# A two-layer image kernel on one core: the reciprocal root from bits and Newton steps, matrix halves made on GpSimd, and the small chains laid out over other half slots

## What is computed

```python
def _gn(v, G=32, eps=1e-5):                     # groups of 4 channels
    g = v.reshape(B_, G, C_ // G, H_, W_)
    m = jnp.mean(g, axis=(2, 3, 4), keepdims=True)
    s = jnp.var(g, axis=(2, 3, 4), keepdims=True)
    return ((g - m) / jnp.sqrt(s + eps)).reshape(v.shape)

# layer 0, of _gn(x)
xh = _conv1x1(x, w_in, b_in)                    # 128 -> 256 channels
pooled = jnp.mean(xh, axis=(2, 3))
hcx = jax.nn.relu(pooled @ kg_w1.T + kg_b1)
kernels = (hcx @ kg_w2.T + kg_b2).reshape(b, c, K, K)
y = conv_general_dilated(x_r, k_r, ...)         # 3x3, each channel its own kernel
y = y * jnp.tanh(jax.nn.softplus(y))            # Mish
return _conv1x1(y, w_out, b_out)                # 256 -> 128 channels

# layer 1, of _gn(x), for each pixel: real FFT over channels, mask, two
# 128 x 128 products, inverse FFT, real part, relu
x = x + layer0(_gn(x))
x = x + layer1(_gn(x))
```

## Time and profile before

| | |
|---|---|
| time, three runs | 3999.41, 4001.52, 4002.96 us (median 4001.52) |
| the profiled execution | 4002.64 us, of which the span of its instructions 4000.8 us |
| busy: PE | 3806.2 us (95%) |
| busy: ACT | 3597.6 us (90%) |
| busy: DVE | 3518.9 us (88%) |
| busy: POOL | 2549.2 us (64%) |
| DMA queues | 30.5% of 16 engines' span |
| chain that ended last | PE 69%, ACT 14%, DVE 8%, issue 5%, POOL 2%, DMA 1% |

### The profile page before, as it was taken

One profiled execution on the slowest core, in us unless ns is written; L12 is line 12 of the kernel. 1 busy time (PEld: TensorE's weight loads), 2 busy tenths in 40 slices (PEclk: granted clock), 3 DMA queues, 4 the chain that ended last, 5 costly groups with the idle time before them and its releaser, 6 DMA issues.

```text
span 4000.8 us, 65640 instructions
## 1 busy us (share of the span) xinstructions
PE 3806.2 (95%) x22348; PEld 2274.3 (57%) x22348; DVE 3518.9 (88%) x4714; ACT 3597.6 (90%) x5827; POOL 2549.2 (64%) x1812
## 2 busy tenths in 40 slices
PE   4899999999999999999999999999999999999998
PEld 2555555555565555655556555555655555555554
DVE  5899989899898988989889898998989889898996
ACT  4889999899998999999999998999989999998885
POOL 2456666666666666666666666666666666666763
PEclk8999999999999999999999999999999999999999
DMA  3212333333333333333333232333323333332222
GB/s 134 59 48 79 111 96 111 100 106 111 96 111 101 106 106 101 111 101 106 101 106 111 96 111 96 111 106 101 111 96 107 104 103 114 97 109 76 74 75 121
DMA packets 111291, 401.85 MB, mean 100 GB/s; under 512 B 13232, under 2 KB 14320, under 8 KB 110704
## 3 DMA queue, kind: packets, MB, share of 16 engines
q1 hardware_dynamic: 110960, 397.66, 30.5%
HBM read 263.39 MB, written 134.22 MB: 99 GB/s over the span
## 4 chain that ended last, share of the span: by engine, by line
PE 69%; ACT 14%; DVE 8%; issue 5%; POOL 2%; DMA 1%; SPq 0%; ACTq 0%; POOLq 0%; DVEq 0%
PE psA L686 31%; PE psBO L732 17%; PE psL L741 9%; ACT tprod L425 4%; DVE accB L929 4%; DVE accS L941 3%; PE psBO L710 2%; PE psBO L712 2%; PE psBO L711 2%; ACT xh L398 2%; ACT tprod L474 2%; PE psBO L721 1%; ACT XS L462 1%; PE psBO L722 1%; PE psBO L723 1%
## 5 line engine op out<-in xcount | busy, mean ns | idle before, releaser
L686 PE MATMUL psA<-hi,wa 128*128 128x288 f16 (+4 forms) x9792 | 1951.5, 282 | 0.8 <-DVE wtmp L911 0.8
L929 DVE SCALAR_TENSOR_TENSOR accB<-xh,vectors,accB 128x1024 f32<-128x1024 f32 x1280 | 1643.6, 1284 | 0.0
L1102 POOL TENSOR_TENSOR tsum<-tsum,tprod 128x1024 f32<-128x1024 f32 x512 | 1209.8, 2363 | 393.8 <-ACT tprod L425 393.5
L941 DVE SCALAR_TENSOR_TENSOR accS<-side,vectors,accS 128x448 f32<-128x448 f32 x2048 | 1403.8, 685 | 22.4 <-ACT accS L434 13.2
L686 PE MATMUL psA<-lo,wa 128*128 128x288 f16 (+5 forms) x4896 | 1330.6, 281 | 0.0
L686 PEld LDWEIGHTS psA<-hi,wa 128*128 128x128 f16 x9792 | 931.4, 98 | 340.3 <-issue 68.9
L732 PE MATMUL psBO<-wm,woutt 128*128 128x512 f32 x2048 | 963.5, 593 | 2.9 <-DVE X L951 2.1
L1106 POOL TENSOR_TENSOR X<-X,zt 128x512 f32<-128x512 f32 x480 | 610.8, 1273 | 485.8 <-DVE accB L929 408.7
L1094 POOL TENSOR_TENSOR lo<-X,hi 128x1024 f16<-128x1024 f32 x256 | 546.8, 2136 | 405.0 <-ACT hi L383 403.6
L732 PEld LDWEIGHTS psBO<-wm,woutt 128*128 128x128 f32 x2048 | 386.5, 190 | 483.0 <-issue 481.9
L425 ACT ACTIVATE tprod<-xh,vectors 128x1024 f32<-128x1024 f32 x512 | 584.0, 1141 | 21.0 <-POOL tsum L1102 18.3
(11 more groups left out here) (166 smaller groups left out, 3582.7 us busy)
## 6 DMA issues: line engine op xcount, KB each, us to landing
X<-in_x_dram SPq DMA_DIRECT2D x256, 512.0 KB, 3.5
out_dram<-X SPq DMA_DIRECT2D x256, 512.0 KB, 2.6
XS<-in_x_dram SPq DMA_DIRECT2D x240, 512.0 KB, 3.5
X<-in_w_t_dram SPq DMA_DIRECT2D x2, 1152.0 KB, 17.7
w1t<-in_w_t_dram SPq DMA_DIRECT2D x1, 256.0 KB, 2.7
wint<-in_w_in_t_dram SPq DMA_DIRECT2D x1, 128.0 KB, 2.3
woutt<-in_w_out_t_dram SPq DMA_DIRECT2D x1, 128.0 KB, 2.6
wm<-in_cos_m_dram SPq DMA_DIRECT2D x1, 64.0 KB, 4.3
```

The lines of the kernel that those rows point to most:

```text
L686: last = mm(o[:, r:r + q, 0:cols], w, src[:, at:at + q, SIDE + dx - 1:SIDE + dx - 1 + cols], start=(tap == ORDER[0] and w is wh and src is ...
L929: V.scalar_tensor_tensor(out=rows_of(accB[:]), in0=xh[:, 8 * j + dy:8 * j + dy + 8, dx:dx + W], scalar=kk[i % 2][:, TAPS + k:TAPS + k + 1] ...
L941: V.scalar_tensor_tensor(out=side_out(), in0=side[:, 8 * j + dy:8 * j + dy + 8, dx:dx + SIDE], scalar=kk[i % 2][:, k:k + 1], in1=side_out( ...
L1102: P.tensor_tensor(tsum[:], tsum[:], tprod[:], ALU.add).then_inc(s_ta, 1)
```

## The change

It has four parts, in words, and then the diff cut to its core.

1. **The reciprocal root.** `stats_rstd` (ACT: Ln, Exp with scale -0.5) is gone. DVE makes a first guess from the bits of the variance (`root_bits`: shift right by one; `root_first`: a constant minus that), and `rstd` on POOL makes three Newton steps in place of one, 15 instructions in place of 7. ACT uses no function outside Mish's table any more.
2. **Halves on POOL.** `weights_high` and `taps_high` (ACT) are gone; POOL copies and subtracts (`weights_halves`, `taps_halves`).
3. **Chains sooner and spread.** The chain of x begins in slot 10. `rstd` and `fold` run at the end of POOL's slot 11; `pooled_products` moves to `small_0` of slot 12 and `hidden` to `small_1` of slot 12; `kernels` to `small_0` and `bias_rows` to `small_1` of slot 13; the three `spread`s to `small_0` and `small_1` of slot 14 and `small_0` of slot 15. For layer 1, `rstd` and `fold_1` move to the end of POOL's slot 2 and `layer1_mean` to `small_0` of slot 3. On POOL `kernel_bias`, and `taps_halves` for the first and third group, stand ahead of the slot's first `tap_add`.
4. **Statistics.** `stat_strips` takes two strips in each of the first six slots, so that the sums of a sample are ready a slot sooner.

```diff
         def stat_strips(n):
-            if n < 5:
+            if n < 6:
                 return (2 * n, 2 * n + 1)
-            return (n + 5,) if n + 5 < STATS else ()
+            return (n + 6,) if n + 6 < STATS else ()
...
-            def stats_rstd(who, i):
-                d = st[who]
-                eng.wait_ge(hk[who + "var"], i + 1)
-                act(d["ln"][:], d["v"][:], ACT.Ln).then_inc(hk[who + "ln"], 1)
-                eng.wait_ge(hk[who + "ln"], i + 1)
-                act(d["r0"][:], d["ln"][:], ACT.Exp, scale=-0.5).then_inc(hk[who + "r0"], 1)
...
-            def taps_high(i, u):
-                eng.wait_ge(s_wt, 3 * i + u + 1)
-                act(wa[:, i % 2, 0, 3 * u * C:3 * (u + 1) * C], wtmp[:], ACT.Copy).then_inc(s_wsh, 1)
-
-            def weights_high(i):
-                eng.wait_ge(s_wn, i + 1)
-                act(wb[:, i % 2, 0, :], wn[:], ACT.Copy).then_inc(s_wbh, 1)
...
+            def root_bits(who, i):
+
+                d = st[who]
+                eng.wait_ge(hk[who + "var"], i + 1)
+                V.tensor_scalar(d["bits"][:], d["v"][:].bitcast(I32), 1, None,
+                                ALU.logical_shift_right).then_inc(hk[who + "bit"], 1)
+
+            def root_first(who, i):
+                d = st[who]
+                eng.wait_ge(hk[who + "bit"], i + 1)
+                V.tensor_scalar(d["r0"][:].bitcast(I32), d["bits"][:], -1.0, ROOT,
+                                ALU.mult, ALU.add).then_inc(hk[who + "r0"], 1)
...
             def rstd(who, i, s):
+
                 d = st[who]
+                k = 15 * i + 2
                 eng.wait_ge(hk[who + "r0"], i + 1)
...
+                for step in range(3):
+                    src = d["r0"] if step == 0 else d["r"]
+                    P.tensor_tensor(d["t"][:], src[:], src[:], ALU.mult).then_inc(s, 1)
+                    eng.wait_ge(s, k + 1)
+                    P.tensor_tensor(d["t"][:], d["t"][:], d["v"][:], ALU.mult).then_inc(s, 1)
+                    eng.wait_ge(s, k + 2)
+                    P.tensor_scalar(d["t"][:], d["t"][:], -0.5, 1.5, ALU.mult, ALU.add).then_inc(s, 1)
+                    eng.wait_ge(s, k + 3)
+                    if step < 2:
+                        P.tensor_tensor(d["r"][:], src[:], d["t"][:], ALU.mult).then_inc(s, 1)
+                        k += 4
+                        eng.wait_ge(s, k)
+                P.tensor_tensor(d["r"][:], d["r"][:], d["t"][:], ALU.mult).then_inc(s, 1)
...
+            def taps_halves(i, u):
+                k, part = 3 * i + u + 1, slice(3 * u * C, 3 * (u + 1) * C)
+                eng.wait_ge(s_wt, k)
+                P.tensor_copy(wa[:, i % 2, 0, part], wtmp[:]).then_inc(s_wsh, 1)
+                eng.wait_ge(s_wsh, k)
                 P.tensor_tensor(wa[:, i % 2, 1, part], wtmp[:], wa[:, i % 2, 0, part], ALU.subtract).then_inc(s_wsl, 1)
...
```

More of the change, by code:

```diff
@@ L520, in slot @@
                 b, s, m = n // STRIPS, n % STRIPS, n - LAG1
-                if s == 11 and b < B - 1:
+                build = b < B - 1
+                if s == 10 and build:
                     moments("x", b + 1)
@@ L527, in slot @@
                     mish_conv(n - 1, 1)
[L528 to L531, removed]
+                if s == 12 and build:
+                    pooled_out(b + 1, small_bank(1))
+                if s == 13 and build:
+                    kernels_out(b + 1, small_bank(1))
+                if s == 3 and b >= 1:
+                    layer1_bias(b - 1, small_bank(1))
                 if n + 2 < N:
                     cast(n + 2)
[L534 to L537, removed]
                 if n >= 2:
@@ L562, in slot @@
                     squares_x(c)
[L563 to L574, removed]
+                if s == 10 and build:
+                    stats_group("x", b + 1, small_bank(0))
+                if s == 12 and build:
+                    hidden_out(b + 1, small_bank(0))
+                if s == 13 and build:
+                    bias_out(b + 1, small_bank(0))
+                if s == 1 and b >= 1:
+                    stats_group("1", b - 1, small_bank(0))
                 if n + 2 < N:
@@ L773, in small_0 @@
                 b, s = n // STRIPS, n % STRIPS
-                if 13 <= s and b < B - 1:
+                if 12 <= s and b < B - 1:
                     eng.wait_ge(s_wa, 2 * n)
+                    if s == 12:
+                        pooled_products(b + 1, small_bank(1))
                     if s == 13:
-                        hidden(b + 1, small_bank(1))
+                        kernels(b + 1, small_bank(1))
                     if s == 14:
-                        bias_rows(b + 1, small_bank(1))
+                        spread(b + 1, 0, small_bank(1))
                     if s == 15:
-                        spread(b + 1, 1, small_bank(1))
+                        spread(b + 1, 2, small_bank(1))
+                if s == 3 and b >= 1:
+                    eng.wait_ge(s_wa, 2 * n)
+                    layer1_mean(b - 1, small_bank(1))
             def bank_1_free(n):
@@ L789, in bank_1_free, with small_1, bank_0_free @@
                 if b < B - 1:
+                    if s == 12:
+                        eng.wait_ge(s_psb, b + 2)
+                    if s == 13:
+                        eng.wait_ge(s_ksb, b + 2)
+                    if s == 14:
+                        eng.wait_ge(s_wt, 3 * (b + 1) + 1)
+                    if s == 15:
+                        eng.wait_ge(s_wt, 3 * (b + 1) + 3)
+                if s == 3 and b >= 1:
+                    eng.wait_ge(s_lb, b)
+            def small_1(n):
+                b, s = n // STRIPS, n % STRIPS
+                if b < B - 1 and s in (10, 12, 13, 14):
+                    eng.wait_ge(s_wa, 2 * n + 1)
+                    if s == 10:
+                        group_moments("x", b + 1, small_bank(0))
+                    if s == 12:
+                        hidden(b + 1, small_bank(0))
+                    if s == 13:
+                        bias_rows(b + 1, small_bank(0))
+                    if s == 14:
+                        spread(b + 1, 1, small_bank(0))
+                if b >= 1 and s == 1:
+                    eng.wait_ge(s_wa, 2 * n + 1)
+                    group_moments("1", b - 1, small_bank(0))
+            def bank_0_free(n):
+                b, s = n // STRIPS, n % STRIPS
+                if n == 0:
+                    eng.wait_ge(s_wt, 3)
+                    return
+                eng.wait_ge(s_wa, 2 * n - 1)
+                if b < B - 1:
+                    if s == 11:
+                        eng.wait_ge(hk["xgsb"], b + 2)
                     if s == 13:
@@ L991, in slot @@
                 if s == 14 and build:
-                    tap_matrices(b + 1, 0, small_bank(0))
-                if s == 15 and build:
-                    tap_matrices(b + 1, 2, small_bank(0))
+                    tap_matrices(b + 1, 1, small_bank(0))
                 tap(n, 6)
```

148 lines of the change are left out of this document (52 added, 96 removed).

## The result

| | before | changed |
|---|---|---|
| median | 4000.66 us (3999.41 to 4002.96) | 3896.98 us (3896.34 to 3897.35) |
| the profiled execution | 4002.64, span 4000.8 | 3897.35, span 3895.3 |
| busy PE, DVE, ACT, POOL | 95, 88, 90, 64% | 97, 90, 89, 68% |

The ratio is 0.974 (95% interval 0.9723 to 0.9757). The forecast was 3902 us, 5 us too high, and inside its range.

A forecast was written before the change was run, and what follows sets the result against it. PE bounds quiet slots at 14.19 us; the five long slots carry ACT's chains. Gains of 86 (samples 1 to 13) + 5 + 2 + 3 + 4 - 0.4 = 99.6 us took 4002.6 to 3903, median 3902; 8-in-10 range 3883 to 3928.

The forecast's parts named there:

- the end: End of the run: two table loads leave, eight instructions come, 0.4 us lost.
- The mean sample: Sample 5's slot changes sum to -5.7 us; with 0.9 for other samples' lower clock, -6.6 for the mean sample.
- the 0.9: Sample 5 is 0.9 us below the mean; taken as lower clock in other samples' slots 2 and 12, which leaves too.
- C + X + 12.8: Length in us of an ACT-bound slot: C is the cast's start, X what is added between cast and second evacuation.
- The root's wait in slot 12: POOL's root ready 2.4 us into slot 12, PE reaches small_0 at 2.08: PE waits 0.3 us.
- ACT's wait for POOL: Slot 13: POOL's first tap_add ends at 11.35, ACT wants its third tap product at 11.0: 0.35 us (bounds 0 and 1.35).
- The 0.3 put for the clock: Slot 13: PE idles about 1.6 us in one piece, which could take its clock down; 0.3 us added.
- PE's clock falls in slot 13: Rival: half clock costs 1.0 to 1.7 us in 14 samples beyond the 0.3; 3915 to 3932 us; chance 0.20.
- The copy: POOL's copy in slot 14, not in the trace: 0.8 us taken, between 0.19 and 1.4; PE bounds the slot anyway.
- Slot 15: One spread and one halving; ACT's 2.35 wait and three copies leave; PE bounds: 14.85 against 16.74 us, -1.9.
- The slower rival, POOL as the bound: Slots 13 to 15: POOL's serial work ahead of the first tap_add makes ACT wait; 4010 us with 4 us copies; chance 0.03.
- the early fetches' waits: ACT waits for PE ahead of its cast, about 2.1 us in slots 3 and 12 and 3.3 in slot 13.

The follow-up runs named there:

- the first experiment: Kernel before with only stats_rstd replaced by the root from bits, rstd in POOL's slots 2 and 12 between cast and first tap_add: 3987.65 us.
- the second: Changed kernel with Ln and Exp back on ACT behind the cast of slots 2 and 11, one Newton step in place of three: 4021.86 us.
- sixth experiments: Kernel before with the root from bits alone, plus 20 unread PE products ahead of product_side in slots 2 and 12: 3965.35 us.
- third experiment: Changed kernel with taps_high and weights_high back on ACT, POOL only subtracting: 3917.34 us.

## Why the prediction was right, point by point

**The sum.** Forecast and measured, by the trace's own parts: samples 1 to 13 gained 92.0 us (86 forecast), sample 14 3.9 (5), sample 15 1.9 (2), sample 0 with the start 7.4 (7), the end 0.4 (-0.4). Together 105.5 of the span, against 99.6. The 7.4 agree in part by luck: the first slot gained 6.1 where the start had 4, slots 12 to 15 of sample 0 gained 4.4 and not 6, and the second strip of statistics cost 2.8 and not 3.2 (in slot 6).

**The mean sample.** -7.26 in the medians against -6.6. By slots, measured (forecast): slot 2 -4.68 (-4.0), 3 +1.52 (+1.4), 10 and 11 together 0.0 (+0.15), 12 -2.74 (-2.1), 13 +1.16 (+1.2), 14 -0.47 (-0.45), 15 -2.07 (-1.9). Slots 2 and 12 gained more mostly because before, most samples lost time to the clock in both; the 0.9 that the prediction put on top of sample 5 for it was the right mechanism, and stands in the medians 18.83 and 18.84 against sample 5's 18.16 and 18.50. In sample 5 itself they gained 4.0 and 2.4; the other 0.3 of slot 12 is the root's wait that did not come.

**Slot length as C + X + 12.8.** It held where ACT is late. Slot 3: C = 1297.53 - 1294.61 = 2.92, sum 15.7, measured 15.70. Slot 12: C = 2.77, X = 0.56, sum 16.1, measured 16.11. Slot 13: C = 4.15, of which the fetch's wait is 3.28, and X = 0.57 + 0.46 + 0.2, sum 18.2, measured 18.16.

**The root's wait in slot 12: 0.3 forecast, none found.** The 15 instructions took 4.94 us (1420.77 to 1425.71) against 3.9 + 1.2 = 5.1, one of them held as supposed (1.29 us for 0.19). But the `tap_add` ahead of them ended 2.97 us ahead of the slot, not 2.7, so the root was ready 1.92 us into the slot and PE came at 2.10. In slot 3 the wait was there: the root was ready at 2.2, and `layer1_mean` came at 2.36 (1296.97 - 1294.61) where 2.08 was PE's own time.

**Slot 13: the total right, two terms off, which is luck.** ACT's wait for POOL was 0.57, not 0.35: POOL's first `tap_add` ended 11.35 us into the slot (1451.25 - 1439.90), which is the forecast to the digit, but ACT wanted its product at 10.89 and not 11.0. The 0.3 put for the clock was not needed: PE idled 1.56 us in one piece, as forecast, and the clock stayed at 1.00. The errors of +0.2 and -0.3 cancel. The rival "PE's clock falls in slot 13" (0.20) did not come about in any of the 15 samples with a chain. The mechanism is real, as the first, second and sixth experiments show. It did not act at 1.5 to 1.6 us of idling in one piece: this slot idled as long, and kept the clock, in samples 1 to 13 of the changed kernel and of the second and third experiment. At 2.0 us it went either way: in sample 0 the slot idled 2.00 us in the changed kernel and kept the clock, and 1.98 with the halves on ACT and lost it.

**The copy: 0.8 taken, 0.504 measured**, and 0.40 for 256 columns. The bound was wide (0.19 to 1.4), and the value near the two-input subtraction of as many columns (0.91) was the wrong neighbour. "GPSIMD Engine Reference" of the Trainium skill, Engine selection, puts one input at about line rate and two at about half the speed of VectorE; the trace fits that, 0.504 us for one input and 0.91 for two, but has no VectorE copy of this form to set beside them. As the prediction said, the time didn't hang on it: slots 14 and 15 have PE as their bound (15.49 and 14.66 of 15.49 and 14.66 us busy).

**Slot 15: 14.67, not 14.85.** The `spread`'s 0.67 was added to 14.19, but slot 15 takes in the sample's edge, as slot 0 does, and slot 0 takes 14.00 with no chain in it. 14.0 + 0.67 is 14.67; that the edge is the cause is an inference from that sum.

**The end: +0.4, not -0.4.** DVE's two and POOL's eight instructions more cost less than two loads and two activations less.

**The slower rival, POOL as the bound** (0.03): not in the changed kernel, but it is what the first experiment shows when the same 15 instructions stand ahead of `tap_add` and not behind the second one: 3.56 us of ACT's time in a slot. The place of `rstd` is what the prediction's slots 3 and 12 rest on, and it priced it at the wait for the root alone. That was right. What it did not say is that the root would be worth next to nothing without that place.

**What was left on the table.** The prediction priced the early fetches' waits about right (C of 2.8, 3.05 and 4.1; measured 2.92, 2.77 and 4.15) and took them as given. Half as much again as the change brought lay in them: 50.8 us, for six moved lines.

## What to carry to other kernels

A small chain has a place on each engine that it passes, and what it costs is the wait that the place causes there, not the work it does: find for each step what is queued behind it on its engine, and put a fetch behind work that doesn't need it rather than ahead of it. When a stall is taken off one engine, look which engine is late next before pricing it, and how long PE idles there, as it can lose its clock; two edits that each win nothing alone (-14 and +21 us here) can be the two halves of one gain (-104). And when the slots of a loop differ, the engine's own work in each slot gives a floor, here 3850 us, that says how much is still to be had.
